# A tail rebuilt as one pipeline over token tiles, with its maxima turned through TensorE and its small-weight statistics moved to the head

## The chip, the cores and the metric

The kernel runs on one core of a Trainium2 chip. The metric is the device time of one execution in microseconds; less is better. Before the change three runs took 1913.91, 1920.22 and 1923.56 us, a median of 1920.22 us.

The engines are TensorE (PE in the profile, its weight loads PEld), VectorE (DVE), ScalarE (ACT), GpSimd (POOL) and SyncE (SP), which here only issues DMAs. Each runs its own list of instructions in order and waits on semaphores. SBUF is the on-chip memory of 128 partitions, PSUM holds the eight banks that TensorE writes.

## The reference

32 sequences of 64 tokens with 1024 channels (2048 tokens) go through an attention branch and a feed-forward branch, each added to its input.

```python
x = x + attn(cond(x, itok_B_0_15, cond_weights), scales_q.., qw_q..)     # 32 heads, 8 KV heads, head size 128, int4 weights
x = x + ffn(cond2(x, itok_B_0_7, ...), W_base, b_base, W_router, A, B)

def cond2(x, ...):                     # x: 32 sequences, 64 rows ("channels") x 1024 columns ("time")
    xm = x * (row < channel_counts)                       # mask of rows, by sequence
    h = gelu(einsum('bct,bch->bht', xm, W_sess[session_ids]) + b)      # 64 -> 128 hidden
    out = einsum('bht,hs->bst', h, W2) + b2                            # 128 -> 64
    return out * (column < seq_lens)
def ffn(x, W_base, b_base, W_router, A, B):
    base = xf @ W_base.T + b_base                          # 2048 x 1024 x 1024
    logits = xf @ W_router.T                               # 8 experts, best two, softmax over them
    h = einsum('td,erd->ter', xf, A)                       # rank 16 for each expert, 128 in all
    lora = einsum('ter,te,eor->to', h, w, B) * 2
    return base + lora
```

## The kernel before

Float32 products are made from float16 parts: an operand is scaled by a power of two, its high half is rounded by ScalarE (a Copy with a scale), the rest is taken by VectorE (scaled operand minus high half), and a product needs three matmuls (high by high, high by low, low by high). The power of two follows from the largest absolute value of the operand, so each operand's maximum must be known before its split: `absmax` reduces along the free axis, GpSimd's `partition_all_reduce` over the partitions, `pow2` makes the scale from the exponent bits.

The work goes in a head (the first conditioning product, maxima, first weights), 8 groups of one KV head (`group`), each of 4 chunks of 512 tokens (`step`), and a tail. A `step` interleaves by hand the projections of the next chunk (`quantum`, `value_block`), the attention of this one (`scores`, `transpose_probs`, `weigh_values`) and the output projection of the last one (`out_quantum` for 8 tiles t and 4 heads h, in two PSUM banks, with a rescale by ScalarE between heads and `add_out` by VectorE at the end). The order is written out for each engine; nothing schedules it.

In the head, VectorE works on the first units of the first chunk and takes the maxima of W_base rows (`absmax(wbmax...)`) between them, from pieces that SyncE loads into two buffers. Then comes `group(0)`.

The tail begins in the last step, chunk 3 of group 7, where no next chunk is left to project. It does, all over 16 tiles of 128 tokens unless said otherwise:

- `turn(k)`, 32 in all: TensorE transposes an eighth of a chunk of the attention's sum y (4 float32 matmuls with the identity); `x1_add(k)` adds the input x, which is loaded again one chunk at a time into the place of turned y (`x_again`), and `x1_max(k)` takes its maximum. Chunk 0 is done in the last step, chunk 1 beside the last output projections, chunks 2 and 3 after them. Only when all 32 are there is the one scale of the hidden layer known (`T_X1`, then the chain of `link` instructions).
- `small_stats`, `small_scales`: maxima and scales of A, the router, W2, W_sess, b_sess, in the last step. Their loads stand behind the last weights on SyncE's list.
- `hidden2(i)`: 4 float32 matmuls (64 rows each) into 4 banks, GELU by ScalarE, split (`h2_hi`, `h2_lo`); `sources(i)`: 48 matmuls; `source_bias` (VectorE), the column mask (GpSimd), `source_lo` and its high part on ScalarE: the split input xf of the feed-forward layer.
- `wf_hi`, `wf_lo`: the 18 pieces of A and W_base are split in between, from two small buffers loaded one by one; W_base's halves land in y's last chunk and in the place of w_out.
- `route_and_lora(i)`: 24 matmuls for the router logits and 24 for the low rank product.
- After all 16 tiles: the routing for all tokens at once (ten dependent VectorE instructions and one Exp), the gates turned by TensorE and multiplied onto the low rank product; and the base layer, 32 half tiles n, each `base(n)` of 24 matmuls of 128x512 and `add_lora(n)` of one float32 matmul, in 4 banks; `base_added` scales and adds, a second instruction adds the bias, and SyncE stores each tile.

The lines that the steps touch: turns L1519, x1_add L833, maxima L544, hidden2 L1712, GELU L1383, h2_hi L1391, h2_lo L1046, sources L1725, source_bias L1060, mask L517, source_hi L1371, source_lo L1068, wf_hi L1366, wf_lo L1051, logits L1738, low rank L1745, routing L1100 to L1118, gates L1785 and L1124, base L1767, add_lora L1772, result L1131 and L1134.

## Time and profile before

| | |
|---|---|
| median of 3 runs | 1920.22 us |
| profiled execution | 1917.04 us, of it span 1915.0 us |
| TensorE busy | 1722.9 us (90%) |
| VectorE busy | 1585.7 us (83%) |
| ScalarE busy | 1394.6 us (73%) |
| GpSimd busy | 55.6 us (3%) |
| mean granted TensorE clock | 0.976 of full |

The span is the time from the first to the last instruction or DMA of the profiled execution. Busy time of TensorE counts modelled matmul spans, which overlap a little at their ends. The page shows each engine's busy tenths in 40 slices of 47.9 us; the last eight are the tail. There TensorE goes from 9 tenths to 7 for five slices and back to 9, while VectorE falls to 2 and ScalarE to nothing in the last four to five.

### The profile page before, as it was taken

How to read it: one execution, taken by the hardware profiler on the slowest of the kernel's cores; microseconds unless marked ns; L12 is line 12 of the kernel's file. 1: busy time of each engine (PE TensorE's matmuls, PEld its weight loads, DVE VectorE, ACT ScalarE, POOL GpSimd, SP SyncE). 2: the span in 40 equal slices, each digit the busy share in tenths (PEclk: the TensorE clock that was granted, in tenths of full speed). 3: DMA queues.
4: the chain of work that ended last, by engine and by line, in shares of the span. 5: the costliest groups of instructions: out<-in, count | busy, mean ns of one | idle time of the engine just before them, and what ended most of it. 6: DMA issues, size and time to landing. Idle time of an engine off the chain costs nothing. (4 is left out here: it accounts for less than half of the span.)

```text
span 1915.0 us, 38654 instructions
## 1 busy us (share of the span) xinstructions
PE 1722.9 (90%) x14306; PEld 942.5 (49%) x14306; DVE 1585.7 (83%) x2670; ACT 1394.6 (73%) x2361; POOL 55.6 (3%) x50
## 2 busy tenths in 40 slices
PE   3689999998999999999989999999999777779999
PEld 3435555544454455445545544454555455554444
DVE  6598999998999899989998998989998868992222
ACT  2568888988888888888888988888988527960000
POOL 0200000000000000000000000000000001320000
PEclk8799999999999999999999999999999978999999
DMA  7321111020103010200111020103020230111111
GB/s 212 100 78 35 34 46 46 1 69 12 46 1 78 4 45 19 61 25 24 34 47 46 2 75 6 46 1 78 12 58 11 89 110 23 40 40 45 44 44 44
DMA packets 118063, 87.67 MB, mean 46 GB/s; under 512 B 13404, under 2 KB 108004, under 8 KB 117860
## 3 DMA queue, kind: packets, MB, share of 16 engines
q1 hardware_dynamic: 117220, 84.83, 15.0%
q8 instruction: 128, 2.10, 0.5%
q14 instruction: 75, 0.61, 0.1%
q10 hardware_dynamic: 640, 0.13, 0.0%
HBM read 76.55 MB, written 8.39 MB: 44 GB/s over the span
## 5 line engine op out<-in xcount | busy, mean ns | idle before, releaser
L1182 ACT ACTIVATE pj<-pj,ratio 128x512 f32<-128x512 f32 x865 | 576.4, 685 | 108.1 <-PE pj L1437 102.3
L1435 PE MATMUL pj<-hid,wts 128*128 128x512 f16 x1024 | 392.1, 383 | 67.1 <-DVE pj L804 25.0
L1437 PE MATMUL pj<-hid,wts 128*128 128x512 f16 x1024 | 390.3, 381 | 0.0
L1191 ACT ACTIVATE sbk<-sbk,wts 128x512 f32<-128x512 f32 x384 | 262.4, 683 | 41.5 <-PE sbk L1504 36.6
L1191 ACT ACTIVATE sa<-sa,wts 128x512 f32<-128x512 f32 x384 | 261.1, 680 | 24.1 <-PE sa L1504 23.9
L1435 PEld LDWEIGHTS pj<-hid,wts 128*128 128x128 f16 x1024 | 99.8, 97 | 237.2 <-ACT pj L1182 72.7
L1447 PEld LDWEIGHTS tp<-wts,hid 128*128 128x128 f16 x3072 | 181.7, 98 | 32.5 <-issue 3.5
L1447 PE MATMUL tp<-wts,hid 128*128 128x128 f16 x3072 | 192.5, 219 | 0.5
L1437 PEld LDWEIGHTS pj<-hid,wts 128*128 128x128 f16 x1024 | 100.6, 98 | 76.6 <-issue 1.1
L704 DVE SCALAR_TENSOR_TENSOR work<-pj,ratio,cos_t 128x512 f32<-128x512 f32 x128 | 95.5, 746 | 45.0 <-PE pj L1437 35.8
L1182 ACT ACTIVATE ex<-ex,ratio 128x512 f32<-128x512 f32 x193 | 128.1, 664 | 3.8 <-PE ex L1437 1.2
L795 DVE SCALAR_TENSOR_TENSOR y<-sa,wts,y 128x512 f32<-128x512 f32 x128 | 95.1, 743 | 27.2 <-PE sa L1504 27.2
L761 DVE TENSOR_TENSOR work<-work 128x512 f32<-128x512 f32 x160 | 109.6, 685 | 1.7
L1502 PE MATMUL sa<-cb,wts 128*128 128x512 f16 x256 | 97.6, 381 | 8.8 <-DVE y L795 6.5
L795 DVE SCALAR_TENSOR_TENSOR y<-sbk,wts,y 128x512 f32<-128x512 f32 x128 | 95.6, 747 | 11.9 <-PE sbk L1504 10.9
L1502 PE MATMUL sbk<-wts 128*128 128x512 f16 x256 | 98.8, 386 | 7.3 <-DVE y L795 7.3
L1502 PE MATMUL sa<-wts 128*128 128x512 f16 x256 | 98.4, 384 | 7.6 <-DVE y L795 7.5
L1502 PE MATMUL sbk<-cb,wts 128*128 128x512 f16 x256 | 97.8, 382 | 4.4 <-ACT sbk L1191 4.4
L714 DVE SCALAR_TENSOR_TENSOR work<-pj,ratio,sin_t 64x512 f32<-64x512 f32 x128 | 96.7, 755 | 4.1
L1435 PE MATMUL ex<-hid,wts 128*128 128x512 f16 x256 | 98.0, 383 | 1.0 <-ACT ex L1182 1.0
L1504 PE MATMUL sa<-wts 128*128 128x512 f16 x256 | 98.3, 384 | 0.0
L1504 PE MATMUL sbk<-wts 128*128 128x512 f16 x256 | 98.2, 383 | 0.0
(243 smaller groups left out, 3184.5 us busy)
## 6 DMA issues: line engine op xcount, KB each, us to landing
wts<-qo_d SPq DMA_DIRECT2D x64, 256.0 KB, 3.2
y<-x_d SPq DMA_DIRECT2D x7, 2048.0 KB, 7.9
wts<-qq_d SPq DMA_DIRECT2D x35, 256.0 KB, 3.1
int_even<-qq_d SPq DMA_DIRECT2D x29, 256.0 KB, 2.9
out_d<-y SPq DMA_DIRECT2D x12, 512.0 KB, 2.6
work<-qv_d SPq DMA_DIRECT2D x16, 256.0 KB, 7.5
work<-sv_d SPq DMA_DIRECT2D x16, 256.0 KB, 9.5
work<-wb_d SPq DMA_DIRECT2D x8, 512.0 KB, 4.4
```

The costliest lines, as they stand in the source:

```text
L704: dve.scalar_tensor_tensor(out=rope_sum_of(u), in0=src, scalar=ratio[:, last:last + 1], in1=tables(cos_t, CB), op0=ALU.mult, op1=ALU.mult)
L714: dve.scalar_tensor_tensor(out=b[0:half], in0=src[half:HD], scalar=ratio[half:HD, last:last + 1], in1=sin_t[half:HD, :].unsqueeze(1).broad ...
L761: dve.tensor_tensor(ra[:, u % 2, :], ra[:, u % 2, :], rb[:, :], ALU.add).then_inc(S["rope_sum"], 1)
L795: dve.scalar_tensor_tensor(out=dst, in0=out_bank[t % 2][:, :], scalar=o_last[:, at:at + 1], in1=dst, op0=ALU.mult, op1=ALU.add).then_inc(y ...
L1182: act.activation(unit_bank[u][:, :], unit_bank[u][:, :], ACT.Copy, scale=ratio[:, KT * u + j:KT * u + j + 1]).then_inc(u_scaled[u], 1)
L1191: act.activation(out_bank[t % 2][:, :], out_bank[t % 2][:, :], ACT.Copy, scale=o_ratio[:, REP * t + h:REP * t + h + 1]).then_inc(o_scaled[ ...
L1435: mm(bank[:, :], w_int[:, u, j, :], hid[:, 0, j, CH * c:CH * (c + 1)], start=j == 0, stop=False, skip_group_check=True)
L1437: mm(bank[:, :], w_int[:, u, j, :], hid[:, 1, j, CH * c:CH * (c + 1)], start=False, stop=True, skip_group_check=True).then_inc(u_done[u], 1)
L1447: last = mm(shared[:, P * i:P * (i + 1)], hid[:, lw, k, CH * c + P * i:CH * c + P * (i + 1)], w_v[:, lh, k, :], start=(k == 0 and (lw, lh) ...
L1502: mm(out_bank[lane][:, :], w_out[:, h, P * t:P * (t + 1)], cbs[c % 2][:, 0, h, :], start=h == 0, stop=False, skip_group_check=True)
L1504: mm(out_bank[lane][:, :], w_out[:, h, P * t:P * (t + 1)], cbs[c % 2][:, 1, h, :], start=False, stop=True, skip_group_check=True).then_inc ...
```

## The change

- **One pipeline.** The loop over 16 tiles now also holds the base layer: in round i, TensorE does the hidden layer of tile i in two halves, the sources of i-1, logits and low rank of i-2, and from i = 4 base half tiles and from i = 6 the gates, `add_lora` and results of tile i-6, one tile behind its base. The last output projections share the loop's first four rounds with the turns of chunk 1 (all new lists of all three engines; `last_step` is a list of its own).
- **Scales by chunk.** The hidden layer's and xf's scales are found for each chunk of 512 tokens: one reduce over 4096 elements (`x1_max(c)`), the column spread over 128 columns, turned by one TensorE matmul (`turn_max`) and reduced along the free axis (`chunk_factors`). GpSimd's reduction over partitions is gone from this place. Routing is done by chunk as well, with four Exp.
- **Head.** The loads and maxima of A, router, W2, W_sess, b_sess now stand between the maxima of W_base and `group(0)`; scales and masks behind the first step. A is loaded twice.
- **W_base in place.** It is loaded whole, in 4 DMAs, into the two chunks of hid that the last group no longer reads, and split into the other two, in 9 pieces of 1024 elements with A, from the last step on.
- **Banks.** Base uses 2 banks, not 4; turns after the eighth use one; hidden2 uses 2. The bias b_base is added to x1 ahead of the base result (`x1_bias`) and no longer behind it. The mask of the session weights moves from VectorE to GpSimd.

```diff
+                             (len_t, len_rep), (seq_t, seq_rep), (row_t, row_of), (tt_t, t_of), (tri_t, tri),
+                             (id32, ident32), (wr_t, w_router_t.rearrange("(k p) e -> p k e", p=P))):
+                sp.dma_start(dst, src).then_inc(S["c2_in"], 16)
+            at[0] = 1024
+            load_stats(w_sess.rearrange("s (q c) d -> (s q) (c d)", q=16), 512, "stats2_in", spare)
+            load_stats(b_sess.rearrange("s (q d) -> (s q) d", q=16), 8, "stats2_in", spare)
             for t in range(2, KT):
                 load_wo(0, t)
             with sp.Fori(1, NKV) as g:
...
+            def projected(c):
+                sp.wait_ge(S["v_done"], NC * (NKV - 1) + c + 1)
+                for u in range(NU):
+                    sp.wait_ge(u_done[u], KT * (NC * (NKV - 1) + c + 1))
+            for half in range(2):
+                projected(half)
+                for l in range(2):
+                    n0 = CH * half + 256 * l
+                    sp.dma_start(hid32[:, l, :, 256 * half:256 * (half + 1)],
+                                 w_base_t[:, n0:n0 + 256].rearrange("(k p) n -> p k n", p=P)).then_inc(wf_in[half], 16)
+            projected(NC - 1)
...
                 dve.wait_ge(S["c2_in"], 16 * 11)
                 absmax(stat[:, T_B2:T_B2 + 1], b2_t)
-                dve.wait_ge(S["stats2_in"], 80)
-                at = 0
-                for n, size in ((T_A, 1024), (T_R, 64), (T_W2, 64), (T_WS, 512), (T_BS, 8)):
-                    last = absmax(stat[:, n:n + 1], spare[:, at:at + size])
-                    at += size
-                last.then_inc(S["stat_c2"], 1)
+                absmax(stat[:, T_R:T_R + 1], small[:, 256:320])
+                absmax(stat[:, T_W2:T_W2 + 1], w2_t)
+                dve.wait_ge(S["stats2_in"], 32)
+                absmax(stat[:, T_WS:T_WS + 1], ws_raw[:, 0:512])
+                absmax(stat[:, T_BS:T_BS + 1], ws_raw[:, 512:520])
+                dve.wait_ge(S["a_in"], 16)
+                absmax(stat[:, T_A:T_A + 1], wb_stage[0]).then_inc(S["stat_c2"], 1)
...
+            def x1_max(c):
+                dve.wait_ge(S["x1_added"], YT * (c + 1))
+                tiles = x1_first if c == 0 else y[:, CT * (c - 1):CT * c, :]
+                absmax(stat[:, T_X + c:T_X + c + 1], tiles.rearrange("p i n -> p (i n)")).then_inc(S["stat_x1"], 1)
+                dve.wait_ge(S["stat_x1"], c + 1)
+                dve.tensor_copy(stat_wide, stat[:, T_X + c:T_X + c + 1].broadcast_to([P, P])).then_inc(S["spread"], 1)
+            def chunk_factors(c):
+                dve.wait_ge(S["max_turned"], c + 1)
+                dve.reduce_max(top[:, T_X + c:T_X + c + 1], max_bank, X).then_inc(S["top_x1"], 1)
+                dve.wait_ge(S["top_x1"], c + 1)
+                m, mx = col(BOUND + c), col(BOUND_X + c)
+                link(dve.scalar_tensor_tensor(out=m, in0=top[:, T_X + c:T_X + c + 1], scalar=float(SEQ), in1=top[:, T_WS:T_WS + 1],
+                                              op0=ALU.mult, op1=ALU.mult))
+                link(dve.tensor_tensor(m, m, top[:, T_BS:T_BS + 1], ALU.add))
...
+            def base_add(n):
+                dve.wait_ge(S["x1_biased"], n // 2 + 1)
+                dve.wait_ge(S["base_done"], n + 1)
+                dve.scalar_tensor_tensor(out=x1_part(n), in0=base_bank[n % 2][:, :], scalar=col(F_BASE + n // YT), in1=x1_part(n),
+                                         op0=ALU.mult, op1=ALU.add).then_inc(S["result"], 1)
             dve.wait_ge(S["consts_in"], 64)
```

The loops of VectorE and TensorE (those of the last step and ScalarE's follow the same cut):

```diff
+            for m, turned in enumerate(((8, 9, 10), (11, 12, 13), (14, 15, None), (None, None, None))):
+                if m:
+                    source_bias(m - 1)
+                h2_lo(m, 0)
+                if turned[0]:
+                    x1_add(turned[0])
+                if m:
+                    source_lo(m - 1)
+                if turned[1]:
+                    x1_add(turned[1])
+                h2_lo(m, 1)
+                if turned[2]:
+                    x1_add(turned[2])
+                add_out(end4, 2 * m)
+                add_out(end4, 2 * m + 1)
+                wf_lo(A_PIECE + 1 + m)
+                if m == 2:
+                    x1_max(1)
+            chunk_factors(1)
+            for i in (4, 5):
+                k = 2 * YT + 4 * (i - 4)
                 x1_add(k)
-                end = x1_max(k)
-            end.then_inc(S["x1_maxed"], 1)
-            dve.wait_ge(S["x1_maxed"], 1)
-            dve.reduce_max(stat[:, T_X1:T_X1 + 1], x1max[:, :], X).then_inc(S["stat_x1"], 1)
-            dve.wait_ge(S["bias_done"], 1)
-            dve.tensor_copy(bias_t, ex[:, 0:B]).then_inc(S["bias_ready"], 1)
...
+            for i in range(6, NT + 2):
+                j = i - 6
+                k = 3 * YT + 2 * (i - 7)
+                if j % CT == 0:
+                    route_gates(j // CT)
+                gate_lora(j)
+                x1_bias(j)
+                base_add(2 * j)
+                base_add(2 * j + 1)
+                if i in (7, 12):
+                    chunk_factors(2 if i == 7 else 3)
+                if i <= NT:
+                    source_bias(i - 1)
...
+            for j in range(NT - 4, NT):
+                if j == NT - 4:
+                    route_gates(NC - 1)
+                gate_lora(j)
+                x1_bias(j)
+                base_add(2 * j)
+                base_add(2 * j + 1)
```

```diff
+            def turn_max(c):
+                pe.wait_ge(S["spread"], c + 1)
+                mm(max_bank, stat_wide, id32, start=True, stop=True).then_inc(S["max_turned"], 1)
...
+            def turn_gates(j):
+                pe.wait_ge(S["route_ready"], j // CT + 1)
+                pe.wait_ge(S["lora_copied"], min(j + 4, NT))
+                need(pe, S["lora_ready"], j)
+                mm(gate_bank, gates[:, j % CT, :, :].rearrange("p e r -> p (e r)"), id32, start=True,
+                   stop=True).then_inc(S["wexp_done"], 1)
             def base(n):
                 c, i, n0 = n // YT, (n // 2) % CT, 512 * (n % 2)
-                if n >= 4:
-                    pe.wait_ge(S["base_added"], n - 3)
+                if n == 0:
+                    pe.wait_ge(S["wf_split"], WF_PIECES)
+                if n < 2:
+                    for lane in range(2):
+                        pe.wait_ge(y_added[lane], CT * NC * NKV)
+                else:
+                    pe.wait_ge(S["result"], n - 1)
                 for k in range(KT):
                     for lx, lw in PARTS:
...
+            for m, turned in enumerate(((8, 9, 10), (11, 12, 13), (14, 15, None), (None, None, None))):
+                hidden2(m, 0)
+                if m:
+                    sources(m - 1)
+                out_pair(m, 0)
+                if turned[0]:
+                    turn(turned[0])
+                out_pair(m, 1)
+                hidden2(m, 1)
+                if turned[1]:
+                    turn(turned[1])
+                out_pair(m, 2)
+                if m == 3:
+                    turn_max(1)
+                if m >= 2:
+                    route_and_lora(m - 2)
+                if turned[2]:
+                    turn(turned[2])
+                out_pair(m, 3)
+            for i in (4, 5):
+                k = 2 * YT + 4 * (i - 4)
+                hidden2(i, 0)
+                turn(k)
+                sources(i - 1)
+                turn(k + 1)
+                hidden2(i, 1)
+                turn(k + 2)
+                route_and_lora(i - 2)
+                base(i - 4)
+                turn(k + 3)
+            for i in range(6, NT + 2):
+                j = i - 6
+                k = 3 * YT + 2 * (i - 7)
+                if i < NT:
+                    hidden2(i, 0)
+                turn_gates(j)
+                if i <= NT:
+                    sources(i - 1)
+                add_lora(2 * j)
+                add_lora(2 * j + 1)
+                if i in (7, 8, 9, 10):
+                    turn(k)
+                base(2 * j + 2)
+                if i < NT:
+                    hidden2(i, 1)
+                if i in (6, 11):
+                    turn_max(2 if i == 6 else 3)
+                route_and_lora(i - 2)
+                if i in (7, 8, 9, 10):
+                    turn(k + 1)
+                base(2 * j + 3)
+            for j in range(NT - 4, NT):
+                turn_gates(j)
+                add_lora(2 * j)
+                add_lora(2 * j + 1)
+                if j + 1 < NT:
+                    base(2 * j + 2)
+                    base(2 * j + 3)
```

Where instructions move, at the three places of which the prediction speaks. First SyncE, at the end of the head; `wb_d` is W_base, `qo_d` the output weights, `a_d` A, the small tensors follow. Before:

```order
L411 DMA id<-id_d 128x128
L368 DMA wts<-soc_d 128x32
L362 DMA wts<-qo_d 128x4x128 x2
L419 DMA work<-wb_d 128x1024 x8
L362 DMA wts<-qo_d 128x4x128 x6
```

Now, from the fifth of the DMAs behind `wb_d` on (`a_d`, `b_d`, `w_d` and one more stand before it):

```order
L445 DMA small<-ids_d 8x32
L445 DMA small<-len_d 128x16
L445 DMA small<-seq_d 128x32
L445 DMA small<-row_d 128x1
L445 DMA small<-t_d 128x8
L445 DMA small<-tri_d 128x64
L445 DMA small<-id_d 128x128
L445 DMA small<-wr_d 128x8x8
L354 DMA wts<-wse_d 128x512
L354 DMA wts<-bse_d 128x8
L382 DMA wts<-qo_d 128x4x128 x6
```

Fourteen DMAs (A, eleven small tensors, two for the statistics) now stand between the last piece of W_base and the rest of the output weights. Next VectorE at the same place, around the last maxima of W_base (`stat<-work`) and the first instructions of `group(0)` (`cos_t`, `vb<-tp`). Before:

```order
L544 TENSOR_REDUCE stat<-work 128x1 x2
L1008 TENSOR_REDUCE stat<-stat 128x1
L704 SCALAR_TENSOR_TENSOR work<-pj,ratio,cos_t 128x512
L722 SCALAR_TENSOR_TENSOR vb<-tp,vb 128x512
L714 SCALAR_TENSOR_TENSOR work<-pj,ratio,sin_t 64x512
```

Now:

```order
L568 TENSOR_REDUCE stat<-work 128x1 x2
L1187 TENSOR_REDUCE stat<-stat 128x1
L568 TENSOR_REDUCE stat<-small 128x1 x3
L568 TENSOR_REDUCE stat<-wts 128x1 x2
L568 TENSOR_REDUCE stat<-work 128x1
L726 SCALAR_TENSOR_TENSOR work<-pj,ratio,cos_t 128x512
L744 SCALAR_TENSOR_TENSOR vb<-tp,vb 128x512
```

Six reductions, three of which wait for those DMAs, now stand ahead of the value split (`vb<-tp`). Last TensorE in the loop over tiles; `cx` and `pj` from `y` are hidden2, `misc` the sources and the logits. Before, a tile:

```order
L1712 MATMUL cx<-y,work 128x512 x2
L1712 MATMUL pj<-y,work 128x512 x2
L1725 MATMUL sbk<-misc,work 128x64 x24
L1725 MATMUL sa<-misc,work 128x64 x24
L1738 MATMUL tp<-misc,hid 128x8 x24
L1745 MATMUL ex<-hid,wts 128x128 x24
```

Now, round i = 7:

```order
L1968 MATMUL pj<-y,work 128x512 x2
L2015 MATMUL tp<-small,cb 128x128
L1985 MATMUL cx<-misc,work 128x64 x48
L2039 MATMUL sa<-wts,work 128x512
L2039 MATMUL sbk<-wts,work 128x512
L1731 MATMUL ex<-small,y 128x128 x4
L2030 MATMUL sa<-hid 128x512 x24
L1968 MATMUL pj<-y,work 128x512 x2
L2001 MATMUL tp<-misc,hid 128x8 x24
L2006 MATMUL tp<-hid,wts 128x128 x24
L1731 MATMUL ex<-small,y 128x128 x4
L2030 MATMUL sbk<-hid 128x512 x24
```

Two base half tiles (L2030) of 24 matmuls and two `add_lora` (L2039) now stand between the small products of a tile.

## Rows read from the trace of the kernel before

**Rows 1.** Windows: core 0, busy us (x instructions) of each engine, clock, DMA share, GB/s

```profile
1590.00:1615.00 25.00, 19.87 (x226) 12.12 (x224) 19.08 (x35) 23.99 (x42) 4.12 (x4) 0.76 0.07 23
...
1665.00:1690.00 25.00, 18.34 (x379) 14.06 (x378) 23.66 (x33) 23.53 (x41) 8.51 (x8) 1.00 0.14 44
1740.00:1765.00 25.00, 25.00 (x108) 11.30 (x107) 8.75 (x13) 0.00 (x0) 0.00 (x0) 1.00 0.16 64
```

**Rows 2.** Chain that ended last: start us, us, engine and work

```profile
1520.77 0.89 PE pj L1519 x8
...
1524.37 7.84 DMA y<-x_d
...
1713.35 10.36 PE cx L1767 x48
...
1741.36 5.18 PE cx L1767 x24
1746.54 0.86 PE cx L1772 x2
```

**Rows 3.** Timeline, VectorE, end of the head: start us, us, line, work [idle before]

```profile
115.44 2.34 DVE L544 TENSOR_REDUCE stat<-work 128x1 f32<-128x1024 f32 x2
...
117.99 0.75 DVE L704 SCALAR_TENSOR_TENSOR work<-pj,ratio,cos_t 128x512 f32<-128x512 f32 x1
```

**Rows 4.** Timeline, TensorE, the first scores

```profile
119.39 0.87 PE L1462 MATMUL tp<-kb,qb 128*128 128x64 f16 x24 [1.46 <-DVE vb L722]
```

**Rows 5.** Timeline, SyncE's DMA issues of the small tensors

```profile
1395.63 0.35 SPq L438 DMA_DIRECT2D small<-b_d  x1
...
1400.37 1.20 SPq L438 DMA_DIRECT2D small<-wr_d  x1
```

**Rows 6.** DMA issues, 1400 to 1409 us: KB each, median us to landing

```profile
wts<-wse_d SPq DMA_DIRECT2D x1, 256.0 KB, 3.2
...
wts<-wr_d SPq DMA_DIRECT2D x1, 32.0 KB, 4.0
```

**Rows 7.** Timeline, VectorE, the last step

```profile
1488.01 0.75 DVE L704 SCALAR_TENSOR_TENSOR work<-pj,ratio,cos_t 128x512 f32<-128x512 f32 x1 [0.28 <-PE pj L1437]
...
1498.72 2.12 DVE L544 TENSOR_REDUCE stat<-wts 128x1 f32<-128x1024 f32 x5
...
1520.81 0.75 DVE L795 SCALAR_TENSOR_TENSOR y<-sbk,wts,y 128x512 f32<-128x512 f32 x1 [2.93 <-PE sbk L1504]
...
1528.15 0.17 DVE L551 TENSOR_SCALAR sc<-bits 128x4 f32<-128x4 f32 x1
```

**Rows 8.** Instructions on one tile (stat): ns min/median/max, first and last start

```profile
L544 DVE TENSOR_REDUCE stat<-y x4: 4409/4420/4420, 12.2 to 58.2; 128x1 f32<-128x4096 f32 x4
```

**Rows 9.** Groups by line and form, 1590 to 1740 us: busy us, mean ns

```profile
L1046 DVE SCALAR_TENSOR_TENSOR work<-cb,sc,work 128x512 f16<-128x512 f32 x32 | 27.5, 918 | 3.4 <-ACT work L1391 3.4
...
L1405 ACT ACT_TABLE_LOAD x1 | 1.3, 1283 | 0.0
```

**Rows 10.** Timeline, TensorE, one tile of the loop

```profile
1645.63 0.86 PE L1725 MATMUL sbk<-misc,qb 128*128 128x64 f16 x24 [1.77 <-DVE pp L1060]
...
1647.02 0.75 PE L1738 MATMUL tp<-misc,hid 128*128 128x8 f16 x24
1647.63 1.50 PE L1745 MATMUL ex<-hid,wts 128*128 128x128 f16 x24
1649.06 0.69 PE L1712 MATMUL cx<-y,work 64*128 64x512 f32 x1
...
1649.60 0.59 PE L1712 MATMUL cx<-y,work 64*128 64x512 f32 x1
```

**Rows 11.** Windows of 5 us where the clock falls

```profile
1530.00:1535.00 5.00, 2.16 (x12) 1.31 (x9) 2.64 (x5) 0.00 (x0) 0.00 (x0) 0.87 0.27 107
1535.00:1540.00 5.00, 2.01 (x5) 0.75 (x6) 3.90 (x7) 0.66 (x1) 0.00 (x0) 0.50 0.00 0
```

**Rows 12.** Timeline, the end of the span

```profile
1911.97 0.33 SPq L489 DMA_DIRECT2D out_d<-y  x1
```

More of the change, by code:

```diff
@@ L518, in _ @@
                                      ALU.mult).then_inc(S["src_ready"], 1)
+            for i in range(NT):
+                mask_source(i)
         @block.vector
@@ new lines, in wf_lo, with h2_lo @@
+            def wf_lo(z):
+                dve.wait_ge(S["wf_hi"], z + 1)
+                dve.scalar_tensor_tensor(out=wf_dst(z, 1), in0=wf_raw(z), scalar=wf_scale(z), in1=wf_dst(z, 0),
+                                         op0=ALU.mult, op1=ALU.subtract).then_inc(S["wf_split"], 1)
+            def h2_lo(i, th):
+                for e in range(2):
+                    n = 4 * i + 2 * th + e
+                    dve.wait_ge(S["h2_hi"], n + 1)
+                    t = slice(512 * th, 512 * th + 512)
+                    dve.scalar_tensor_tensor(out=h2[i % 2][:, 1, e, t], in0=g32[:, e, :], scalar=col(SH2 + i // CT),
+                                             in1=h2[i % 2][:, 0, e, t], op0=ALU.mult, op1=ALU.subtract).then_inc(S["h2_split"], 1)
@@ L1525, in step @@
+            def step(p4, ahead, out4):
                 if ahead:
@@ L1672, in group @@
             def group(g, first=False, last=False):
-                def nothing(t):
-                    pass
                 for c in range(NC):
-                    step((g, c), (g, c + 1) if c + 1 < NC else (None if last else (g + 1, 0)),
-                         None if first and c == 0 else (g, c - 1), turn if last and c == NC - 1 else nothing)
+                    if last and c == NC - 1:
+                        last_step((g, c), (g, c - 1))
+                    else:
+                        step((g, c), (g, c + 1) if c + 1 < NC else (g + 1, 0), None if first and c == 0 else (g, c - 1))
             pe.wait_ge(S["consts_in"], 64)
```

735 lines of the change are left out of this document (425 added, 310 removed).

## The prediction

> **What bounds the kernel now.** I read the windows first, since the page's slices show only that the tail is uneven. While the layers of small products run, TensorE is busy 18 of 25 us and VectorE and ScalarE nearly all of the time; later, from 1740 us, TensorE is busy 25 of 25 and the others stand nearly still [rows 1]. So two stretches with opposite limits lie behind one another. The chain of waits says where the second begins: base runs from 1713.35 us to the end, 5.18 us for a half tile's 24 matmuls and 0.86 for its low rank part [rows 2]. Ahead of it three loads of x, of 7.5 to 7.9 us, stand in the chain with nothing beside them, the first at 1524.37 [rows 2].
>
> TensorE's own work from 1488.0 us (where VectorE enters the last step [rows 7]) is short of the 427 us that pass to the end. For one tile: hidden layer 4 x 0.43 = 1.73 (the steps between its starts; two matmuls of 64 rows run beside each other), sources 1.39, logits 0.61, low rank 1.43 [rows 10], a gate 0.22 (a quarter of a turn's 0.89 [rows 2]), base and low rank part 2 x 6.04. That is 17.5 us, 280 for 16 tiles. 32 turns take 28.5, 64 output quanta of two 512-column matmuls (0.43 each, by base's 5.18/24) 27.6, the last attention step 4. In all 340 us. 87 us of the tail is what a perfect pipeline could win.
>
> **The change, part by part.** I go by the times of the profiled execution (1917.04 us, 2.0 of it outside the span); the median of the three runs is 3.2 us above it, and I don't add that.
>
> *Head.* VectorE starts the first step at 117.99 us, right behind the last maximum, and TensorE's first scores wait for its value split until 119.39 [rows 3, 4]. Now six reductions stand between, and their data is ordered late: A can be requested only when the seventh piece of W_base is read, at 116.6 (half of the pair that starts at 115.44). SyncE needs 4.7 us from the first of the eleven small tensors to the start of the eleventh [rows 5], so the router's load is issued at 121.9, and lands 4.0 us later as its twin did [rows 6], at 125.9. W_sess is issued at 123.1 + 0.5 and lands 3.2 later [rows 6], at 126.8. Then reductions of 512 and 1024 elements, 0.7 + 1.2 (half of 2.34 [rows 3]), so VectorE goes on at 128.8 and not at 118.0: 10.8 us. Nothing covers it: three quanta of the next chunk stand before the scores on TensorE, then all of them wait, and ScalarE with them. Scales and masks behind the first step are 10 small instructions of 0.2 [rows 7], 1.2 us beyond what is hidden. I take 12. Bounds: 2 if the wait were hidden and only the reductions counted, 16 if TensorE falls to its lower clock and works twice as long for a few us behind the gap.
>
> *Last step.* VectorE sets its end, at 1528.3 now [rows 7]. Out go 2.1 us of statistics [rows 7], eight maxima of 0.6 and the scales, 8 in all; in come one reduce of 4.4 [rows 8], sixteen scalar instructions of 0.19 = 3.1, five splits of 1024 elements and 0.7 of small ones. A split of 512 takes 0.66 alone and 0.92 beside GpSimd [rows 9]; twice that less the start is 1.2 to 1.8, and I take 1.3 since GpSimd is idle there. Together +6.8, less 3 us of idle that the new order fills (2.9 stood before one add [rows 7]). End at 1532.
>
> *First four tiles.* VectorE has 10.6 us per tile: two source_bias, two source_lo and two add_out of 0.66, four h2_lo of 0.88 (they run beside the masks), three x1_add of 0.6, one split of 1.3. ScalarE has 10.0. But both go through one circle, since g32 now holds only half a tile: GELU pair, output rescale, h2_hi, h2_lo, GELU of the second half, and ScalarE's list puts output rescales that wait for TensorE inside. Adding that circle up I get 12.2 us, so 48.8; the bounds are VectorE's 10.6 and, with a mask and a whole float32 turn inside the circle too, 15. With the one maximum of 4.4 and the factors of 3.1, both on VectorE: 1588.4.
>
> *Tiles 4 and 5.* 13.9 us of TensorE each (the products, four turns, one base half tile), 2.3 of them done while it waited: 25.5, to 1613.9.
>
> *From round 6 on* TensorE has all that is left: ten hidden layers 17.3, 16 gates 3.5, 11 sources 15.3, 30 base half tiles 155.4, 32 low rank parts 27.5, 12 logits and low rank products 24.5, eight turns 7.1; sum 250.6. VectorE's 10 us and ScalarE's 7 per round of 17.5 lie beside it. Of a pair of low rank parts the second (0.86) covers the add (0.75) that frees the first's bank. Where it does wait: in round 6 for the first routing, which is queued behind the last x1_add: 12 instructions, those of 32 elements at 0.2 like the scalar ones, those of 256 at 0.4 (the fixed part and a fourth of a 1024 reduction's 1.2 [rows 3]), about 4 us; again in round 6 for `turn_max(2)`, because VectorE reduces 4.4 us behind source_lo, 5 us; rounds 7, 10 and 14 and the last gates 6.5. I take 15.5; none of it needs to come (0), and if each of the 15 pairs also waited 1 us for its bank it would be 30.
>
> *Table loads.* The change makes 4 Exp out of 1, each between GELUs. A table load takes 1283 ns [rows 9]. There are eight in place of two, for GELU and Exp in turn; the first stands in the last step as now, the second is in my 4 us of round 6, and the other six lie beside base products, 7.7 us on ScalarE, which has 10 us to spare in each round. The Trainium skill ("ScalarE: Activation LUTs", What ACT_TABLE_LOAD costs) adds a drain of about 1.4 us to each switch. By it the stall of round 6 would be some 1.4 us longer (an estimate from that page). The load's own length agrees with the trace; no row I read shows the drain, and the sum goes by the row.
>
> *Loads.* The three waits for x go: each chunk is now requested a round or more before its first add. W_base comes in behind the session weights, some 30 us before the last step.
>
> *Clock.* After 2.4 us without work TensorE was granted 0.5, its lower level of 1.2 GHz, for the next window of 5 us [rows 11]. I expect two or three such falls (end of the last step, round 6), 2 to 3 us each where it is on the path: 6.
>
> *End.* The last store is issued at 1911.97, 3.0 before the end [rows 12]; one add of 0.75 stands before it, no longer the bias: 3.9 behind the last matmul, with waits.
>
> Sum: 1613.9 + 250.6 + 15.5 + 6 + 3.9 + 12 = 1901.9, and 2.0 outside: 1904 us, 0.8% under the median. The tail gives 25 us, the head takes 12 back.
>
> **Rivals.**
> *The pipeline flows.* Four tiles at VectorE's 10.6, no stall in round 6, no low clock: 6.4 + 15.5 + 6 less, 1876. For it speaks that the present loop shows VectorE 95% busy, so waits of its kind do vanish [rows 1]. Against it, the three lists wait for one another inside half a tile.
> *The head's wait is hidden.* If the small loads are there when VectorE arrives: 10 to 12 less, 1892. Against it speaks only arithmetic of issue times.
> *The wait for two banks.* If VectorE is late with the adds (it stands behind the bias add of 1.2 and whatever the last round left), each pair of base products starts 1 us late: 15 more, 1919, no change.
> *Slower: the lower clock.* From 1488 to 1614 TensorE has 89 us of work in 126. If it stays at 1.2 GHz there (0.76 was granted on average in the worst of today's windows [rows 1]), that is 178 and the stretch is TensorE's: 52 more, 1956. It decides once over half of that stretch is at the lower level; from there the kernel is slower than before. Base itself would hold the full clock, as it does at 1740 [rows 1].
>
> **Numbers.** Forecast 0.44, flow 0.15, hidden head 0.12, two banks 0.19, lower clock 0.10. A run of this kernel can tell 0.5% from no change: under 1910.6 is faster, over 1929.8 slower. The forecast's own error is some 10 us (the circle of the four tiles above all), so a fifth of it lies above 1910.6: faster 0.35 + 0.15 + 0.12 + 0.03 = 0.65; slower 0.10 and 0.02 for two banks with a longer head; the same 0.23. The range reaches from the flow case to between two banks and the lower clock: 1878 to 1926.
>
> **What would show it.** In the new profile: an idle time of VectorE of 8 to 10 us near 118 us, put down to a DMA, with TensorE's scores behind it; if it isn't there, the second rival holds. The last step's VectorE list ending 44 us after it began. Gaps on TensorE before `tp<-small,cb` and before the small `ex` matmul of round 6. From there to the end TensorE busy over 95%, 17.5 us a round, 19.2 with turns; a gap at every second base product means two banks. The windows between last step and round 6 show whether the clock is 0.8 or 0.5. I am wrong if the four first tiles take over 15 us each, or under 11.

## The result, and the profile after

The changed kernel takes 1914.89 us (median of 20 runs, 1911.26 to 1916.93), the kernel before, in 20 runs beside it, 1921.81 us. The ratio is 0.9966, with a 95% interval of 0.9956 to 0.9975: 0.34% less, where 0.8% was forecast (1904 us against the median of 1920.22). The profiled execution has a span of 1913.9 us; that of before had 1915.0.

The windows first, the same stretches as in [rows 1]; columns are busy us (x instructions) of PE, PEld, DVE, ACT and POOL, the granted clock, DMA share, GB/s.

```profile
1590.00:1615.00 25.00, 18.51 (x200) 12.96 (x198) 18.46 (x37) 11.81 (x20) 4.55 (x4) 0.93 0.07 22
1665.00:1690.00 25.00, 23.80 (x205) 13.67 (x202) 15.78 (x34) 7.74 (x13) 2.50 (x2) 1.00 0.06 23
1740.00:1765.00 25.00, 24.94 (x222) 12.99 (x220) 14.59 (x16) 7.84 (x13) 2.50 (x2) 1.00 0.05 22
```

The two opposite stretches are one: at 1740 us TensorE is still busy all the time, but VectorE is now busy 14.6 of 25 us beside it instead of 8.8, and the 1665 window has gone from 18.3 to 23.8 us of TensorE. The pipeline that the change wanted is there.

The head, VectorE's timeline (start, length, engine, line, operation, idle time and what ended it), against [rows 3]:

```profile
124.82 0.47 DVE L568 TENSOR_REDUCE stat<-small 128x1 f32<-128x64 f32 x3 [6.02 <-DMA small<-wr_d]
126.31 0.75 DVE L568 TENSOR_REDUCE stat<-wts 128x1 f32<-128x512 f32 x2 [1.02 <-DMA wts<-bse_d]
126.98 1.21 DVE L568 TENSOR_REDUCE stat<-work 128x1 f32<-128x1024 f32 x1
128.11 0.74 DVE L726 SCALAR_TENSOR_TENSOR work<-pj,ratio,cos_t 128x512 f32<-128x512 f32 x1
```

VectorE waits 6.02 us for the router's load, the last of the eleven, and 1.02 for the session bias, and enters the first step 10.1 us later than before (128.11 against 117.99). TensorE's first scores follow at 129.50, against 119.39 [rows 4]:

```profile
129.50 1.46 PE L1670 MATMUL tp<-kb,qb 128*128 128x64 f16 x24 [10.92 <-DVE vb L744]
```

TensorE has stood for 10.92 us by then, and comes out of it at the lower level of its clock, so that the same 24 matmuls take 1.46 us where they took 0.87:

```profile
125.00:130.00 5.00, 0.49 (x10) 0.50 (x11) 3.95 (x9) 0.00 (x0) 0.72 (x2) 0.50 0.10 32
```

The shift stays through the eight groups. The value splits (one in each step) stand 10.1 us later in the first step, 9.8 us at the smallest, near 1050, and 12.4 us in the last group's third step, and then this happens, VectorE and GpSimd in one stretch:

```profile
1463.24 4.10 DVE L791 TENSOR_TENSOR work<-work,rmax 128x512 f32<-128x512 f32 x1
1467.26 0.68 DVE L787 TENSOR_TENSOR qb<-work,qb 128x512 f16<-128x512 f32 x1
```

```profile
1462.89 3.90 POOL L531 TENSOR_TENSOR work<-work,misc 128x2048 f32<-128x2048 f32 x1 [1333.88 <-DMA work<-wse_d]
```

An instruction that takes 0.68 us elsewhere takes 4.10, as long as GpSimd multiplies the session weights by their mask. The next value split is 2.5 us later still (14.9 behind that of before), and the last step begins at 1503.54 us instead of 1488.01 [rows 7].

From there to round 6 things go as worked out. VectorE's list of the last step ends 43.0 us after its start (44 forecast), and the first routed round begins 126.7 us after that start (125.9). In round 6 TensorE has the two waits that were expected:

```profile
1635.22 0.79 PE L2015 MATMUL tp<-small,cb 128*128 128x128 f32 x2 [3.83 <-DVE cb L947]
1635.81 2.77 PE L1985 MATMUL cx<-misc,qb 128*128 128x64 f16 x48
...
1652.38 0.80 PE L1738 MATMUL ex<-small,work 128*128 128x128 f32 x2 [4.38 <-DVE work L862]
...
1653.66 2.72 PE L2006 MATMUL tp<-hid,wts 128*128 128x128 f16 x24
```

Behind each of them the products take nearly twice their time (the sources 2.77 us and not 1.56, the low rank 2.72 and not 1.50), while the clock was granted at its lower level of 1.2 GHz for part or all of the window:

```profile
1635.00:1640.00 5.00, 4.78 (x52) 3.92 (x53) 1.65 (x3) 1.13 (x2) 0.00 (x0) 0.50 0.48 197
...
1650.00:1655.00 5.00, 2.62 (x40) 2.56 (x41) 3.61 (x4) 0.52 (x1) 0.00 (x0) 0.65 0.00 0
```

After one more wait, of 1.20 us in round 7, TensorE waits no longer than 0.06 us at a time until round 17. Round 8 (the dots stand for logits, low rank and the second turn) and the first line of round 9:

```profile
1683.93 1.13 PE L1968 MATMUL pj<-y,work 64*128 64x512 f32 x4
1684.99 0.49 PE L2015 MATMUL tp<-small,cb 128*128 128x128 f32 x2
1685.32 1.56 PE L1985 MATMUL cx<-misc,qb 128*128 128x64 f16 x48
1686.71 1.10 PE L2039 MATMUL sa<-wts,work 128*128 128x512 f32 x2
1687.65 1.02 PE L2039 MATMUL sbk<-wts,work 128*128 128x512 f32 x2
1688.51 1.05 PE L1731 MATMUL ex<-small,y 128*128 128x128 f32 x8
1689.40 5.34 PE L2030 MATMUL sa<-hid 128*128 128x512 f16 x24
1694.68 1.13 PE L1968 MATMUL pj<-y,work 64*128 64x512 f32 x4
...
1698.64 5.34 PE L2030 MATMUL sbk<-hid 128*128 128x512 f16 x24
1703.91 1.13 PE L1968 MATMUL pj<-y,work 64*128 64x512 f32 x4
```

There is no idle time in it, and yet it takes 19.98 us, not the 19.2 forecast. Each half of a hidden layer takes 1.06 us from its start to the next one's start (the prediction had 0.865), the gate 0.33 instead of 0.22. From round 11 on there is no turn; there the second low rank part takes 1.08 us to the next start and not 0.86. In the last five rounds each gate is also followed by a wait:

```profile
1894.68 1.12 PE L2039 MATMUL sa<-wts,work 128*128 128x512 f32 x2 [0.51 <-DVE work L955]
1895.64 1.02 PE L2039 MATMUL sbk<-wts,work 128*128 128x512 f32 x2
1896.72 5.35 PE L2030 MATMUL sa<-hid,y 128*128 128x512 f16 x24
```

### The profile page after: what moved, and what is told of

Same layout as the page of the kernel before. It is cut to its first block and busy times, and to the rows that moved or that the text cites. A ratio compares the mean times of both kernels' runs of the same rounds, so it can differ in the third digit from the quotient of the medians.

```text
span 1913.9 us, 38885 instructions
## 1 busy us (share of the span) xinstructions
PE 1729.1 (90%) x14314; PEld 937.1 (49%) x14314; DVE 1598.4 (84%) x2715; ACT 1407.5 (74%) x2372; POOL 61.3 (3%) x50
## 3 DMA queue, kind: packets, MB, share of 16 engines
q1 hardware_dynamic: 117732, 84.76, 14.9%
## 5 line engine op out<-in xcount | busy, mean ns | idle before, releaser
L1320 ACT ACTIVATE sa<-sa,wts 128x512 f32<-128x512 f32 x384 | 260.8, 679 | 15.6 <-PE sa L1712 15.5
L1710 PE MATMUL sbk<-wts 128*128 128x512 f16 x256 | 98.8, 386 | 11.7 <-DVE y L817 7.1
```

Source lines behind the costliest of these rows:

```text
L1320: act.activation(out_bank[t % 2][:, :], out_bank[t % 2][:, :], ACT.Copy, scale=o_ratio[:, REP * t + h:REP * t + h + 1]).then_inc(o_scaled[ ...
L1710: mm(out_bank[lane][:, :], w_out[:, h, P * t:P * (t + 1)], cbs[c % 2][:, 0, h, :], start=h == 0, stop=False, skip_group_check=True)
```

## The experiments

Each was timed beside the kernel before; the diffs are shortened. Ratios are to that kernel, with 95% intervals; the changed kernel's is 0.9966. "x us from the changed kernel" is the difference of the two ratios times 1921.8, and is uncertain by some 3 us, so that small effects rest on the traces.

**late_stats** takes the wait out of the head; the work stays.

```diff
             dve.reduce_max(stat[:, T_WB:T_WB + 1], wbmax, X).then_inc(S["stat_wb"], 1)
-            small_stats()
...
                 def first_out_scales(what, n):
                     out_scales(what, n)
                     if what == "end":
-                        small_scales()
-                        masks()
+                        small_stats()
+                def first_factors(what, n):        # chunk 1 of the first group
+                    if what == "end":
+                        small_scales()
+                        masks()
```

> The changed kernel with VectorE's six small reductions moved from ahead of the first attention step to its end, and the four scales and the masks from that step's end to the next one's. Theory (the head's wait for the small operands lies wholly on the path, and the reductions themselves nearly so): VectorE enters the first step at 118.6 us instead of 128.1, and gets 2.4 us of reductions back in a step where it is over 90% busy; 7 to 9 us less than the changed kernel's 1914.9, that is 1906 to 1908. Rival (the steps after the head make up for a late start anyway, and the missing gain was lost in the tail): 1913 to 1916, and the last step begins at about 1503 us as before.

Measured: 1903.91 us, 0.9926 (0.9912 to 0.9941), 7.7 us from the changed kernel. VectorE goes on at once, and the reductions stand at the first step's end without a wait:

```profile
118.26 0.75 DVE L726 SCALAR_TENSOR_TENSOR work<-pj,ratio,cos_t 128x512 f32<-128x512 f32 x1
...
156.81 0.75 DVE L568 TENSOR_REDUCE stat<-wts 128x1 f32<-128x512 f32 x2
```

So the wait is on the path (7.04 us of idle time on VectorE against 7.7 us), and the rival falls.

**early_loads** leaves VectorE's order alone and issues the 13 small loads between W_base's.

```diff
+            early = [(dst, src, "c2_in") ...]      # the eleven, and two of "stats2_in"
             for k in range(WB_STATS):
...
                 sp.dma_start(wb_stage[k % 2], w_base_t[P * k:P * (k + 1), :]).then_inc(wb_in[k % 2], 16)
+                for dst, src, name in (early[3 * (k - 2):3 * (k - 1)] if k >= 2 else ()):
+                    sp.dma_start(dst, src).then_inc(S[name], 16)
```

> The changed kernel with SyncE's 13 small loads issued between the last six loads of W_base instead of behind them; order of VectorE's work unchanged. Theory (what costs in the head is the wait for landings, not the reductions): VectorE's 6.0 and 1.0 us of idle time go, what is left is a wait for A alone, issued at 117.5 us and landing some 4 us later, so about 2 us; 4 to 6 us less than 1914.9, that is 1909 to 1911. Rival (13 issues of 0.4 us between the W_base loads make these late, and VectorE waits there instead): no gain, 1914 to 1917.

Measured: 1905.89 us, 0.9937 (0.9921 to 0.9953), 5.6 us less. What is left is A's own wait:

```profile
121.07 1.22 DVE L569 TENSOR_REDUCE stat<-work 128x1 f32<-128x1024 f32 x1 [1.69 <-DMA work<-a_d]
```

**head_only** is the opposite: the kernel before with the head part alone (SyncE's 14 loads and `small_stats()` behind W_base as in the changed kernel, `small_scales()` at the first step's end).

> The kernel before with the head part of the change alone: the loads of A, of the small tensors and of the session weights behind W_base, the six small reductions ahead of the first attention step, the four scales at that step's end; the tail as it was. Theory (the head costs the whole wait, and taking it back by itself gained 7.7 us of the changed kernel's 1914.9): VectorE resumes near 128 us instead of 118.0, 2 to 3 us of statistics leave the last step; 7 to 10 us over the kernel before, a ratio of 1.0035 to 1.005. Rival 1 (the head's price in the prediction, 12 us, with nothing back in the last step): 1.006 or more. Rival 2 (the wait is made up for later, and what late_stats gained came from the new place of the statistics): under 1.002.

Measured: 1925.74 us, 1.0047 (1.0032 to 1.0062): 9.0 us over the kernel before, with the same wait (6.06 us, then 0.69):

```profile
124.50 0.47 DVE L542 TENSOR_REDUCE stat<-small 128x1 f32<-128x64 f32 x3 [6.06 <-DMA small<-wr_d]
```

The whole change is 6.5 us under the kernel before and its head alone 9.0 over it, so all the rest of it is worth 15.5 us, if the two parts add.

**mask_twice** doubles GpSimd's product.

```diff
             gp.tensor_tensor(ws, ws, cm_t...broadcast_to([P, NT, HID]), ALU.mult).then_inc(S["wsess_masked"], 1)
+            gp.wait_ge(S["wsess_masked"], 1)
+            gp.tensor_tensor(ws, ws, cm_t...broadcast_to([P, NT, HID]), ALU.mult).then_inc(S["wsess_masked"], 1)
```

> The changed kernel with GpSimd's product of the session weights and their mask done twice in a row, which leaves the output as it is. Theory (while GpSimd runs its 3.9 us on 2048 elements, VectorE's instruction stands still, as the one of 4.10 instead of 0.68 us at 1463.2 us showed): a second such VectorE instruction behind the first and a last step that begins 2 to 3.5 us later; 1917 to 1918.5. Rival (the 2.4 us lost in that step come from W_base's four loads at the same time, or are chance): one long instruction as before, 1914 to 1916.

Measured: 1917.44 us, 0.9988 (0.9975 to 1.0), 4.2 us over the changed kernel. Two instructions of VectorE are held up, one behind the other:

```profile
1459.91 4.09 DVE L793 TENSOR_TENSOR work<-work,rmax 128x512 f32<-128x512 f32 x1
1463.93 4.09 DVE L789 TENSOR_TENSOR qb<-work,qb 128x512 f16<-128x512 f32 x1
```

```profile
1459.71 3.76 POOL L531 TENSOR_TENSOR work<-work,misc 128x2048 f32<-128x2048 f32 x1 [1330.78 <-DMA work<-wse_d]
1463.54 3.93 POOL L533 TENSOR_TENSOR work<-work,misc 128x2048 f32<-128x2048 f32 x1
```

From the value split of the last group's third step to that of its last step pass 50.7 us here, 45.1 in the changed kernel and 42.2 in the two runs that follow, where GpSimd has no such product. The second product adds more than its own length; the granted clock behind it was 0.50 (1467 to 1472 us).

**mask_scalar** and **mask_slots** take the product from GpSimd and give it to ScalarE.

```diff
-            gp.tensor_tensor(ws, ws, cm_t...broadcast_to([P, NT, HID]), ALU.mult)...
+            def mask_sessions(n):
+                for i in range(CT * n, CT * (n + 1)):
+                    act.activation(ws[:, i, :], ws[:, i, :], ACT.Copy, scale=cm_t[:, i:i + 1])...
```

> The changed kernel with the product of session weights and mask taken from GpSimd (2048 elements, 3.9 us at 1462.9) and done by ScalarE as 16 copies of 128 elements with the mask as scale, four at a time in the last step. Theory (GpSimd's instruction holds VectorE's up, which costs 2.4 us in the last group's third step; ScalarE has 12 of 43 us free in the last step): no VectorE instruction of 4.1 us, last step begins 2 to 3 us earlier, 1911.5 to 1913. Rival (the 16 copies, about 4 to 5 us, put ScalarE behind in the last step, whose splits VectorE waits for): 1914 to 1918.

Measured: 1911.84 us, 0.9959 (0.9944 to 0.9974), 1.3 us less, which the intervals don't tell from nothing. The trace shows both theory and rival at work: no long instruction, the last step begins 42.2 us after the step before it instead of 45.1, but then VectorE waits 2.81 us, where it waited 1.22 in the changed kernel, for an output sum that ScalarE rescaled late:

```profile
1525.05 0.75 DVE L814 SCALAR_TENSOR_TENSOR y<-sbk,wts,y 128x512 f32<-128x512 f32 x1 [2.81 <-PE sbk L1720]
```

> The changed kernel with the session mask done by ScalarE as in mask_scalar, but only eight of the 16 copies in the last step, together in the 2.8 us for which ScalarE waits there for TensorE, and the others in rounds 6 and 9, where it is busy 7 to 9 us of 20. Theory (taking the 3.9 us from GpSimd gives VectorE 2.5 to 3 us back, and mask_scalar lost half of it to a wait of 2.8 us behind the copies): 2.4 to 3 us less than 1914.9, 1912 to 1912.5. Rival (the last step does not gain from VectorE's earlier start, since something else sets its end): 1914 to 1915.

Measured: 1908.60 us, 0.9953 (0.9939 to 0.9966), 2.5 us less, the size expected. The eight copies fill ScalarE's gap, of which 0.50 us is left:

```profile
1503.01 2.44 ACT L1515 ACTIVATE work<-work,misc 128x128 f32<-128x128 f32 x8
```

**turn_max_later** moves one matmul.

```diff
-                if i in (6, 11):
-                    turn_max(2 if i == 6 else 3)
+                if i == 11:
+                    turn_max(3)
...
                 base(2 * j + 3)
+                if i == 6:
+                    turn_max(2)
```

> The changed kernel with TensorE's turn of the third chunk's maxima moved from the middle of round 6 to its end, behind the logits, the low rank and a half tile of base. Theory (TensorE stands 4.38 us for VectorE's 4.4 us maximum and comes out of it at the lower clock): both go, 4 to 6 us less than 1914.9, 1909 to 1911. Rival (the wait only moves, since the scales that the maximum gives are needed for the first turn of round 7, where there already was a wait of 1.2 us): 1913.5 to 1915, with a longer idle time before the turn of round 7.

Measured: 1904.66 us, 0.9930 (0.9917 to 0.9944), 6.9 us less. The wait is gone and not replaced: the one before the first turn of round 7 was 1.20 us and is 1.20. The clock's fall went with it (the low rank takes 1.50 us instead of 2.72):

```profile
1643.46 1.50 PE L2006 MATMUL tp<-hid,wts 128*128 128x128 f16 x24
...
1649.98 0.38 PE L1738 MATMUL ex<-small,work 128*128 128x128 f32 x2
```

**round_order**: `sources(5)` ahead of `turn_gates(0)` in round 6, and in the last rounds `turn_gates(j + 1)` between `base(2 * j + 2)` and `base(2 * j + 3)`.

> The changed kernel with two orders of TensorE changed: in round 6 the sources before the first gate, and in the last four rounds the gate of the next tile between its two base products instead of behind them. Theory (TensorE is the bound from round 6 on, so each wait of its own that is covered comes off the end): of the 3.82 us before the first gate 1.4 go, 2.8 while the clock is low there, and three of the five waits of 0.51 us at the end, 1.5; 1911 to 1913. Rival (a wait at round 6 only moves to the first gate's product on VectorE, and the clock's dip follows whatever wait is left): 1914 to 1915.

Measured: 1907.62 us, 0.9939 (0.9923 to 0.9955), 5.2 us less, more than expected. The wait before the first gate is 2.32 us (a new one of 0.60 follows), and three of the five waits of 0.51 at the end are gone. What I had not counted is that the clock's fall there would go too: behind 3.83 us of idle time it fell to 0.50 for the window shown above, behind 2.32 it did not fall:

```profile
1630.00:1635.00 5.00, 2.08 (x19) 1.26 (x16) 3.95 (x10) 3.63 (x5) 0.00 (x0) 1.00 0.93 377
1635.00:1640.00 5.00, 4.94 (x22) 1.94 (x21) 4.88 (x6) 0.82 (x2) 2.50 (x2) 1.00 0.26 105
```

The length of the wait alone does not decide it: in the kernel before the clock fell behind 2.4 us without work [rows 11], and in the changed kernel behind 2.66 us at 474.

**hidden_single** takes apart the two matmuls of 64 rows, in rounds 7 to 15.

```diff
-                    hidden2(i, 0)
+                    hidden2(i, 0, (0,))
                 turn_gates(j)
+                    hidden2(i, 0, (1,))
...
+                    hidden2(i, 1, (0,))
                 base(2 * j + 2)
-                    hidden2(i, 1)
+                    hidden2(i, 1, (1,))
```

> The changed kernel with the hidden layer's two matmuls of 64 rows, which stand beside each other in each half, taken apart in rounds 7 to 15: the gate between the first two, one half tile of base between the others. Theory (two such matmuls run beside each other only while they follow directly, and each series pays its beginning and end: a half takes 1.06 us in the trace, a whole layer of four took 1.73 in the kernel before): a single one takes 0.75 to 0.9 us, so 3.0 to 3.6 us a tile instead of 2.12, over nine tiles 8 to 13 us more, 1923 to 1928. Rival (they don't run beside each other, 1.06 is two times 0.53): no change, 1914 to 1916.

Measured: 1932.07 us, 1.0068 (1.0047 to 1.0089), 19.6 us over the changed kernel, far more than expected. A single matmul takes the 1.06 us that the pair took:

```profile
1711.14 1.12 PE L1968 MATMUL pj<-y,work 64*128 64x512 f32 x2
1712.19 5.35 PE L2030 MATMUL sa<-hid 128*128 128x512 f16 x24
```

Nine tiles with two such times more are 19.1 us. So the pair is wholly parallel: one such matmul standing alone costs as much as two beside each other. The Trainium skill ("TensorE: Matmul & The Clock Gate", Why this matters for your kernels) says of matmuls with 32 rows that a single one takes the same time as one with 128, and that the gain is the tiles' running at once. The trace agrees for 64 rows: 1.06 us for one or for two, and 0.86 to 1.08 for a low rank part of 128 rows.

**grouped** puts the second hidden half directly behind the low rank parts (`hidden2(i, 1)` ahead of `base(2 * j + 2)` in rounds 7 to 15).

> The changed kernel with the second half of the hidden layer moved, in rounds 7 to 15, from behind the first base product of the round to directly behind the low rank parts (or their turn), so that TensorE's float32 matmuls follow one another and each of nine rounds has one change from float32 to float16 less. Theory (what made TensorE's own work from round 6 on 261 us instead of the 250.6 of the prediction is a surcharge of 0.1 to 0.2 us at each change of kind: a hidden half 1.06 instead of 0.865 us, a gate 0.33 instead of 0.22, a second low rank part 1.08 ahead of base and 0.86 ahead of a turn): 0.2 to 0.3 us a round, 2 to 3 us in all, 1912 to 1913. Rival (the surcharge belongs to the hidden layer, not to the change): 1914 to 1916, with 1.06 us for each half and 1.08 for the second low rank part.

Measured: 1911.98 us, 0.9962 (0.9949 to 0.9975), 0.8 us less: no difference that can be told. The trace says why:

```profile
1743.95 1.10 PE L2039 MATMUL sa<-wts,work 128*128 128x512 f32 x2
1744.89 1.02 PE L2039 MATMUL sbk<-wts,work 128*128 128x512 f32 x2
1745.84 1.13 PE L1968 MATMUL pj<-y,work 64*128 64x512 f32 x4
1746.90 5.35 PE L2030 MATMUL sa<-hid 128*128 128x512 f16 x24
```

The half still takes 1.06 us with float32 of 128 rows ahead of it. Only the low rank part gains (0.95 instead of 1.08), in the rounds without a turn. My theory, a surcharge at each change between float32 and float16, holds for the low rank part and falls for the hidden half.

**combined** is late_stats, turn_max_later, mask_scalar and round_order together; **combined2** has mask_slots for mask_scalar, grouped, and the first turn of round 7 behind `base(4)`.

> The changed kernel with the edits of late_stats, turn_max_later, mask_scalar and round_order together. If each removes time from one path of its own, in its stretch, the sum is 7.7 and 6.9 (measured against the kernel before: ratios 0.9926 and 0.9930, the changed kernel's 0.9966) and 2.4 and 2 (expected): 19 us under 1914.9, 1894 to 1899. Rival (after the clock's dip is gone in round 6 or the head is shorter, another wait takes its place): over 1901.

> The edits of late_stats, turn_max_later, round_order, grouped and mask_slots together, and the first turn of round 7 behind a base product, since it waited 1.2 us for VectorE's scales. The first combination was 1893.0; if each new edit adds its own: 1.5 for the mask's copies in the gap, 2.7 for the kinds, 1.2 for the turn, 1887 to 1890. Rival (the new order makes the hidden half wait for ScalarE's gelu of the first half): 1892 to 1895, with idle time ahead of the second hidden half.

Measured: combined 1892.99 us, 0.9861 (0.9841 to 0.9882), 20.2 us under the changed kernel; the four alone sum to 21.1. Combined2 1884.74 us, 0.9827 (0.9811 to 0.9844), 26.7 us under the changed kernel and 1.7% under the one before; both came out somewhat faster than expected. In the window from 1590 us on, which had 18.5 us of TensorE and a clock of 0.93 in the changed kernel, combined2 has:

```profile
1590.00:1615.00 25.00, 25.00 (x254) 16.81 (x254) 14.15 (x21) 11.90 (x19) 3.12 (x4) 1.00 0.01 1
```

## Why the prediction was half right

The sum missed the changed kernel's span by 12.0 us (1901.9 against 1913.9), and by its own steps this goes as follows.

*Head: right.* 12 us were priced, 10.1 measured at the first step, and 9.0 for the whole part by head_only. The lower clock behind the wait, which the prediction named only for its upper bound, did come, and the 9.0 hold it. The arithmetic of issue times was within 1 us of the landings (125.9 forecast, 124.82 measured; 126.8 and 126.3). The rival of a hidden wait falls.

*The way to the last step: a term was missing.* It starts 15.5 us later than before where 12 were priced. 2.5 of it are GpSimd's product, which the prediction did not price at all, though its row of splits beside GpSimd (0.92 us instead of 0.66 [rows 9]) hinted at it; mask_twice and the 2.9 us that both runs without the product give back in that step show it. The Trainium skill ("SBUF — State Buffer", Who interferes with whom) has the rule: a VectorE instruction with two inputs in SBUF contends with a GpSimd instruction that reads SBUF, and the lock on the ports that they share is exclusive. The trace agrees, 4.10 us beside 3.90. It need not be an instruction with two inputs, though: in early_loads, grouped and turn_max_later the one held up was a cast of 0.42 us with one, here in early_loads:

```profile
1454.58 3.77 DVE L775 CAST qb<-work 128x512 f16<-128x512 f32 x1
```

Another 0.7 comes from the new order of the last step's first instructions. The other 12.4 are 10.1 from the head and 2.3 that came for the most part in three jumps, each beside a short fall of the clock in one of the two executions. The shift goes from 10.4 to 12.3 us between the value splits at 476 and 524 us of the changed kernel (clock 0.83 from 475 to 485), from 11.5 to 9.8 between those at 1003 and 1050 of the kernel before (its clock 0.83 from 1002 to 1012), and from 10.4 to 12.0 across this window of the changed kernel:

```profile
1192.00:1202.00 10.00, 8.49 (x53) 3.94 (x54) 6.07 (x10) 6.59 (x12) 0.00 (x0) 0.83 0.01 3
```

In the seven other runs with the same head the shift at that point was 7.1 to 11.7 us. So these 2.3 are in the main how the two profiled executions happened to fall, and not a cost of the change; no run tests it by itself.

*Last step, four tiles, tiles 4 and 5: right.* For the last step 43.0 us against 44; 12.4, 12.5, 13.2 and 10.9 us for the four tiles, against 12.2 each; together 126.7 against 125.9. The flow rival (10.6 a tile) and the slower clock (the windows of 25 us from 1540 to 1665 have 0.84 to 0.93, not half) did not come.

*From round 6 on: here it failed.* The term "TensorE's own work, 250.6" was too small. From 1630.2 us to the end TensorE is busy 267.2 us, of which the two falls of the clock take 5.2 (the products behind the waits less their usual times; 6 forecast), so 262.0, 11.4 more than priced. By kinds, from the steps between starts in full-speed rounds: 20 hidden halves of 1.06 are 21.2 and not 17.3; the low rank parts, 1.80 a pair ahead of a turn and 2.02 ahead of base, are 31.4 and not 27.5; 16 gates some 5.0 and not 3.5; base, 5.28 ahead of a hidden half and 5.19 else, 157 and not 155.4; the logits and low rank products 1.1 less. That is 10 of the 11. The mistake was to price each kind by the inner step of a long series: the hidden layer's 4 x 0.43 was read between starts within a series of eight records, and its first step (1649.06 to 1649.60 [rows 10]) is 0.54. The change cuts such series to halves and puts another kind behind each: the two steps of a half take 0.53 us each (starts at 1683.93 and 1684.46, the gate at 1684.99). This is read from the steps in the traces. The runs bear on it from two sides: hidden_single, which cuts the halves once more, pays another 1.06 us for each single matmul, and grouped gains 0.13 on a low rank part, while no run puts a hidden layer together again.

*Stalls: mostly right in place, 2.9 us too dear.* 3.83, 4.38, 1.20 and five of 0.51, 12.0 in all, and 0.6 scattered, against 15.5; rounds 10 and 14 had none. The end is 3.9 as priced. For a base bank TensorE waited 0.06 us, in ten of the rounds, and not 1 us, so the rival of the two banks falls: round 8 has no idle time before either product.

3.5 (the way to the last step) + 0.8 (to round 6) + 11.4 (TensorE's own work) - 0.8 (clock) - 2.9 (stalls) = 12.0, which is the miss. "The tail gives 25 us" became 15.5, "the head takes 12 back" 9.0.

*Table loads.* The one for the routing's Exp is issued at 1624.89, and that for the GELU behind it stands in the first wait of round 6. The extra drain of the Trainium skill ("ScalarE: Activation LUTs", What ACT_TABLE_LOAD costs) does not show; ScalarE's timeline there:

```profile
1624.61 0.26 ACT L1506 ACTIVATE work<-tp 128x128 f32<-128x128 f32 x1
1624.89 1.28 ACT L1511 ACT_TABLE_LOAD   x1
1632.11 0.23 ACT L1511 ACTIVATE work<-work 128x32 f32<-128x32 f32 x1 [5.93 <-DVE work L934]
1632.35 1.28 ACT L1478 ACT_TABLE_LOAD   x1
1633.65 1.26 ACT L1478 ACTIVATE cb<-pj,small 128x512 f32<-128x512 f32 x2
```

Each load begins within 0.03 us of the end of the instruction ahead of it, and the GELU within 0.02 of the load's. The measurement decides: a switch cost 1.28 us here.

## What to carry to other kernels

Work that is moved out of a tail has to be put where its data already is: the same reductions cost 9 us as a wait in front of the first step and some 1.3 at its end (an estimate: 9.0 for head_only less 7.7 back in late_stats, uncertain by some 3). When the engine that bounds a stretch is sized from a trace, take for each kind of work the time from its start to the start of the next kind, in a series as long as the new one will be; the inner step of a longer series leaves out what every cut adds. And an instruction for an idle GpSimd is not free where VectorE is the bound.

## What the hardware showed that was not expected

- GpSimd's product of 2048 elements (3.6 to 3.9 us) held up one VectorE instruction each time, in every run that has it: one of 0.68 us took 4.10, or a cast of 0.42 took 3.7 to 3.8.
- A float32 matmul of 64 rows and 512 columns takes 1.06 us to the next kind, alone or as a parallel pair; in the longer series of the kernel before, the first step was 0.54 [rows 10] and the inner ones 0.43.
- 3.83 and 4.38 us without work on TensorE were followed by a clock of 0.50 and 0.65; of shorter waits some were (2.66 us at 474, 0.83 from 475 to 485) and some were not (2.32 us in round_order). Removing such a wait gave back more than its length (6.9 us for 4.38), as the products behind it no longer ran slow.
